# Two causal attentions in a two-layer network: row maxima by 64 queries, and turns moved by one chunk

## The reference

```python
scores = (einsum(q_cos, k_cos) + einsum(q_sin, k_sin)) / sqrt(8) * exp(log_scale)   # layer 0
scores = einsum('bhqd,bhkd->bhqk', q, k) / sqrt(8)                                    # layer 1
scores = where(causal, scores, -inf)
attn = softmax(scores, axis=-1)          # over 512 keys, exact maximum of each row
out = einsum('bhqk,bhkd->bhqd', attn, v) @ Wo.T
```

## Time and profile before

| | |
|---|---|
| runs | 1258.14, 1243.11 and 1254.38 us, median 1254.38 |
| the profiled execution | 1254.72 us, its span 1253.1 us |
| busy over the span | PE 79%, DVE 66%, ACT 54%, POOL 47% |
| `attend0`, from about 393 to 640 us | PE 225.8 of 247.0 us, DVE 224.5, ACT 185.0, POOL 114.1 |
| `attend1`, 973 to 1253 us | PE 246.3 of 280.0 us, DVE 233.6, ACT 195.0, POOL 183.8 |

### The profile page before, as it was taken

The page is one execution under the profiler, slowest core; times in us unless marked ns, Lnnn a source line. Parts: engine busy times, 40 slices in busy tenths (PEclk is TensorE's granted clock), DMA queues, the critical chain, the costliest instruction groups (busy, mean ns, idle before and its releaser), DMA issues. The chain is left out here.

```text
span 1253.1 us, 25971 instructions
## 1 busy us (share of the span) xinstructions
PE 996.1 (79%) x8908; PEld 650.2 (52%) x8908; DVE 832.1 (66%) x1875; ACT 680.5 (54%) x1293; POOL 586.7 (47%) x862
## 2 busy tenths in 40 slices
PE   3789753989874999999976463499999699999997
PEld 1456531777672455555533332388888345555542
DVE  1566331799986899999927666133333799999992
ACT  1266443776720777777755353122222377777774
POOL 3467537244432444455433466111110477777774
PEclk9899766899996899999997575699999599999998
DMA  4322032477775222222202233466664111112110
GB/s 135 110 49 54 27 100 89 139 206 201 217 156 132 70 70 70 70 73 77 61 7 63 76 106 96 146 183 192 190 184 136 43 45 53 53 53 53 53 47 27
DMA packets 151525, 122.57 MB, mean 98 GB/s; under 512 B 31712, under 2 KB 134032, under 8 KB 151408
## 3 DMA queue, kind: packets, MB, share of 16 engines
q1 hardware_dynamic: 141664, 102.89, 29.6%
q0 software_dynamic: 8016, 17.71, 4.9%
q10 hardware_dynamic: 1728, 0.46, 0.2%
HBM read 75.75 MB, written 42.61 MB: 94 GB/s over the span
## 5 line engine op out<-in xcount | busy, mean ns | idle before, releaser
L2103 ACT ACTIVATE attend_probs<-attend_attend_ps 128x512 f32<-128x512 f32 x640 | 353.7, 600 | 152.7 <-PE attend_attend_ps L2171 141.5
L2171 PE MATMUL attend_attend_ps<-attend_q,attend_ks 50*128 50x512 f16 (+3 forms) x1024 | 236.6, 307 | 23.1 <-ACT attend_probs L2103 20.3
L2070 POOL TENSOR_SCALAR_AFFINE_SELECT attend_probs<-attend_probs 128x512 f32<-128x512 f32 x256 | 159.6, 636 | 196.7 <-ACT attend_probs L2103 196.1
L2139 PE MATMUL attend_attend_ps<-attend_ks,attend_q 48*128 48x512 f16 (+3 forms) x1024 | 191.5, 317 | 27.8 <-DMA attend_ks<-k_stack 20.2
L2184 PE MATMUL attend_attend_ps<-attend_probs,attend_vals 128*32 128x512 f32 (+3 forms) x2048 | 183.2, 455 | 0.0
L2266 DVE TENSOR_REDUCE attend_neg_max<-attend_attend_ps 128x2 f32<-128x1024 f32 x128 | 155.5, 1215 | 14.3 <-PE attend_attend_ps L2151 9.0
L2151 PE MATMUL attend_attend_ps<-identb,stairs 64*128 64x128 bf16 (+1 forms) x1280 | 144.5, 213 | 0.0
L2171 PEld LDWEIGHTS attend_attend_ps<-attend_q,attend_ks 50*128 50x128 f16 x1024 | 70.4, 94 | 121.6 <-ACT attend_probs L2103 73.7
L2268 DVE TENSOR_REDUCE attend_neg_max<-attend_attend_ps 128x2 f32<-128x768 f32 x128 | 121.9, 952 | 8.2 <-PE attend_attend_ps L2151 7.3
L2151 PEld LDWEIGHTS attend_attend_ps<-identb,stairs 64*128 64x128 bf16 x1280 | 104.4, 100 | 19.3 <-issue 4.7
L1886 PE MATMUL experts_experts_ps<-experts_rowsT,experts_w_in 128*128 128x256 f32 (+1 forms) x468 | 110.2, 386 | 1.6 <-ACT experts_rowsT L1835 1.5
(11 more groups left out here) (316 smaller groups left out, 1933.4 us busy)
## 6 DMA issues: line engine op xcount, KB each, us to landing
experts_w_in<-in_L_ffn_w_dram SPq DMA_DIRECT2D x78, 176.0 KB, 2.4
q_stack<-middle_parts SPq DMA_DIRECT2D x24, 256.0 KB
k_stack<-middle_parts SPq DMA_DIRECT2D x24, 256.0 KB
attend_q<-q_stack SPq DMA_DIRECT2D x64, 96.0 KB
attend_ks<-k_stack SPq DMA_DIRECT2D x64, 96.0 KB
middle_w_in<-in_L_ffn_W_dram SPq DMA_DIRECT2D x23, 256.0 KB
middle_w_out<-in_L_ffn_W_dram SPq DMA_DIRECT2D x23, 256.0 KB
experts_rows<-sorted POOLq DMA_DIRECT2D x39, 128.0 KB, 2.5
```

Source lines behind the costliest of these rows:

```text
L2070: pool.affine_select(out=block_, in_=block_, compare_op=ALU.is_ge, fill=0.0, base=0, pattern=[[0, GH], [1, P]], channel_multiplier=-1).the ...
L2103: act.activation(probs[:, u.par, 2 * c + side, :], ps[:, PROB + side, :], ACT.Exp, scale=SCALE ** -2)\
L2139: pe.matmul(ps[:, bank + side, col:col + (qt + 1) * P], q[rows(side, KR), g, pair, qt * P:(qt + 1) * P], ks[rows(side, KR), g, pair, 0:(qt ...
L2171: mm = pe.matmul(ps[:, PROB + side, col:col + S - kt * P], ks[rows(side, KM), g, pair, kt * P:(kt + 1) * P], q[rows(side, KM), g, pair, kt ...
```

## The change

Maxima by 64 queries. Query blocks are now of `H` = 64 (`QS` = 8 a head). A block of 64 queries fills 64 of PE's columns, so a matmul of `maxima` fills a quarter of the array (64 rows by 64 columns); the four heads of the unit go to the four quarters. The two sides of one pair write the two partition halves of one and the same bank. A chunk covers one large and one small block of all four heads instead of one of two heads: 1024, 1024, 1024, 1024 and 512 elements a partition for DVE, where there were five times 1024. The mask's products are one instead of two per head and chunk. Each matmul of `probabilities` is now two, each with 64 of the 128 keys, into two partition halves of one bank. The layout of the maxima and their parts follows; the turn of the maxima is two matmuls instead of one.

Turns. PE turns the maxima of unit t - 1 in chunk 0, and the mix of unit t - 4 in chunk 1, behind the first piece of `mix`. DVE's copy of the maxima comes after the reduction of chunk 0, its `divide` after chunk 1's, and `add_row` moves from the end of a step to behind `split_maxima` of the next.

POOL. The copy of the values and the gathers of the feed-forward result stood before a unit's four masks, and the joins after them; now a gather and a join stand after the first mask, and the copy for the next unit, the second gather and the second join after the last.

```diff
         def max_chunk(c):
-            if c == 4:
-                return [(0, 1, 0), (1, 1, 256)]
-            return [(c // 2, 3, 0)] if c % 2 == 0 else [(c // 2, 2, 0), (c // 2, 0, 384)]
+            if c == 0:
+                return [(QS - 1, 0)]
+            return [(QS - 1 - c, 0), (c - 1, (QS - c) * H)] if c < 4 else [(3, 0)]
+        def half(side, pair):
+            first = H * ((side + pair) % 2)
+            return slice(first, first + H)
...
-            for n in range(UNITS + JOIN_AFTER * layer):
-                if n < UNITS:
...
+            copy_values(0)
+            for n in range(UNITS):
+                mask(n, 0)
+                gather(n, 0)
                 if layer == 1 and n >= JOIN_AFTER:
-                    join_branches(n - JOIN_AFTER)
+                    join_branch(n - JOIN_AFTER, 0)
+                for i in range(1, QT):
+                    mask(n, i)
+                if n + 1 < UNITS:
+                    copy_values(n + 1)
+                if layer == 1:
+                    gather(n, 1)
+                    if n >= JOIN_AFTER:
+                        join_branch(n - JOIN_AFTER, 1)
...
                 blocks = max_chunk(c)
-                for n, (pair, qt, col) in enumerate(blocks):
+                for n, (qs, col) in enumerate(blocks):
+                    for pair in range(HP):
+                        for side in range(2):
+                            pe.matmul(ps[half(side, pair), bank + pair, col:col + (qs + 1) * H],
+                                      q[rows(side, KR), g, pair, qs * H:(qs + 1) * H], ks[rows(side, KR), g, pair, 0:(qs + 1) * H],
+                                      start=(n == 0), stop=False)
...
                 for pair, kt, col in prob_chunk(c):
-                    mm = pe.matmul(ps[:, PROB + side, col:col + S - kt * P], ks[rows(side, KM), g, pair, kt * P:(kt + 1) * P],
-                                   q[rows(side, KM), g, pair, kt * P:S], start=True, stop=True)
+                    for first in (0, H):
+                        mm = pe.matmul(ps[first:first + H, PROB + side, col:col + S - kt * P],
+                                       ks[rows(side, KM), g, pair, kt * P + first:kt * P + first + H], q[rows(side, KM), g, pair, kt * P:S],
+                                       start=True, stop=True)
                 mm.then_inc(prob_ps.sem, 1)
...
+            def before_maxima(t):
+                if active(t, 5, UNITS):
+                    pe.wait_ge(context_done.sem, context_done.done(t - 5))
+                    if (t - 5).group == NG - 1:
+                        pe.wait_ge(added.sem, added.done((t - 5).row))
             def before_mix(t):
-                if active(t, 2, UNITS):
-                    pe.wait_ge(maxT_ready.sem, maxT_ready.done(t - 2))
-                elif active(t, 5, UNITS):
-                    pe.wait_ge(context_done.sem, context_done.done(t - 5))
-                if active(t, 5, UNITS) and (t - 5).group == NG - 1:
-                    pe.wait_ge(added.sem, added.done((t - 5).row))
-            def before_maxima(t):
-                if active(t, 4, UNITS):
-                    pe.wait_ge(context_done.sem, context_done.done(t - 4))
-                elif active(t, 2, UNITS):
-                    pe.wait_ge(maxT_ready.sem, maxT_ready.done(t - 2))
+                if active(t, 1, UNITS):
+                    pe.wait_ge(maxT_ready.sem, maxT_ready.done(t - 1))
+                else:
+                    before_maxima(t)
             def step(t):
                 row_ends = active(t, 4, UNITS) and (t - 4).group == NG - 1
                         maxima(t, c)
                     if active(t, 2, UNITS):
                         probabilities(t - 2, c, 1)
-                    if c == 0 and active(t, 4, UNITS):
-                        before_mix(t)
-                        turn_mix(t - 4)
+                    if c == 0 and active(t, 1, UNITS):
+                        before_maxima(t)
+                        turn_maxima(t - 1)
                     if 1 <= c <= 3 and active(t, 3, UNITS):
                         mix(t - 3, c - 1)
                         if c == 3:
                             mix(t - 3, 3)
-                    if c == 1 and active(t, 1, UNITS):
-                        before_maxima(t)
-                        turn_maxima(t - 1)
+                    if c == 1 and active(t, 4, UNITS):
+                        before_mix(t)
+                        turn_mix(t - 4)
                     if c == 2 and row_ends:
-                        if active(t, 1, UNITS):
-                            pe.wait_ge(maxT_ready.sem, maxT_ready.done(t - 1))
                         turn_context(t - 4)
...
             def reduce(u, c):
                 dve.wait_ge(scored.sem, scored.after(u, 2 * c + 1))
                 first = max_pair(u, c)
                 pair_banks = ps[:, first:first + 2, :]
-                out = neg_max[:, u.par, :, :, :]
-                if c == 4:
-                    ins = dve.tensor_reduce(out[:, :, :, 1], pair_banks.rearrange("p s (h t) -> p s h t", h=HP), X_AXIS, ALU.max,
-                                            negate=True)
-                elif c % 2 == 0:
-                    ins = dve.tensor_reduce(out[:, :, c // 2, 3], pair_banks, X_AXIS, ALU.max, negate=True)
-                else:
-                    dve.tensor_reduce(out[:, :, c // 2, 2], pair_banks[:, :, 0:384], X_AXIS, ALU.max, negate=True)
-                    ins = dve.tensor_reduce(out[:, :, c // 2, 0], pair_banks[:, :, 384:512], X_AXIS, ALU.max, negate=True)
+                for qs, col in max_chunk(c):
+                    ins = dve.tensor_reduce(neg_max[:, u.par, :, qs], pair_banks[:, :, col:col + (qs + 1) * H], X_AXIS, ALU.max, negate=True)
                 ins.then_inc(maxed.sem, 1)
...
             def step(t):
                 if active(t, 1, UNITS):
                     split_maxima(t - 1)
+                if active(t, 5, UNITS) and (t - 5).group == NG - 1:
+                    add_row(t - 5)
                 for c in range(MCH):
                     if active(t, 0, UNITS):
                         reduce(t, c)
-                    if c == 0 and active(t, 4, UNITS):
+                    if c == 0 and active(t, 1, UNITS):
+                        copy_maxima(t - 1)
+                    if c == 1 and active(t, 4, UNITS):
                         divide(t - 4)
-                    if c == 1 and active(t, 1, UNITS):
-                        copy_maxima(t - 1)
-                if active(t, 4, UNITS) and (t - 4).group == NG - 1:
-                    add_row(t - 4)
```

110 lines of the change are left out of this document (55 added, 55 removed).

## The result

The changed kernel takes 1307.56 us (median of 1298.23 to 1309.54), the kernel before 1251.57 in the same comparison: ratio 1.046 (1.041 to 1.050). The forecast was 1270 us, with a range of 1252 to 1293. The profiled execution took 1306.94 us, its span 1305.3, 52.2 more than before.

A forecast was written before the change was run, and what follows sets the result against it. The closed PE-ACT loop was taken as the bound, DVE's loop having hardly more slack. `attend0` +12.0, `attend1` +3.9, first steps -2.6 and `attend1`'s extra +2 made +15.3 on 1254.72: 1270 us, range 1252 to 1293.

The forecast's parts named there:

- POOL: nothing: POOL's new order of gathers, joins and copies: claimed to cost nothing, each mask being used one step later.
- off the new loop: `attend1`'s delays from DVE's slower split, late `divide` and turn: claimed off the new loop, so its row is also 31.82 us.
- Nothing below is a matter of the clock: PE's granted clock, 1.00 in the steady part of both attentions before: claimed to play no part, no time counted.
- the forecast's +15.3: Whole kernel: the summed slowdown in us, added to the profiled execution's 1254.72.
- The closed loop through PE and ACT, not DVE, is the bound: A step of `attend0`: PE and ACT waiting on each other sum to 7.23 us, the whole step, without slack.
- Transposes +0.55, from 1.03 to 1.58: From `mix`'s first piece to chunk 2: the moved transposes lengthen this stretch of the loop by 0.55 us a step.
- Quarters run side by side, -0.05: Maxima in chunk 3: quarter-array matmuls run side by side, fewer columns saving 0.05 us a step on the loop.
- the step of 7.73: New normal step in us, claimed for both attentions: 7.23 + 0.55 - 0.05.
- End of a batch row 0.90: End of each four-step batch row: 0.59 us for the context's transposes plus 0.31 for the projection, 1.18 before.
- the whole extra of 1.16 us a row: `attend1`'s longer row before the change, put down to DVE's slower split; a quarter, +2 us, was kept on the loop.
- First three steps -2.6: First three steps of each attention, without a mix: DVE sets the pace and saves 6 x 0.43 us.
- two sides in one bank: Rival, chance 0.25: lower rows' maxima need 0.21 us more in chunks 2 and 3; step 8.15, kernel 1294 us.

The follow-up runs named there:

- the first trace: The changed kernel unaltered, as first profiled, against the kernel before: ratio 1.046, rows of 33.2 us in `attend0` and 34.5 in `attend1`.
- e2: The changed kernel with PE's and DVE's order of the turns put back as before; ratio 1.000 to the kernel before.
- e3: The kernel before with only the turns moved as in the change (PE's and DVE's order); ratio 1.052 to the kernel before.
- e5: The changed kernel unaltered, run again on chip 6; ratio 1.037 to the kernel before on that chip.
- e14: The changed kernel with plain DMAs in place of the indirect gathers, on chip 13; ratio 1.025 to the kernel before.
- e12: The changed kernel with the mix's four transposes also issued in chunk 0, ahead of the turn of the maxima; ratio 1.048 to the kernel before.
- e6: The kernel before, unaltered, on chip 6 as the reference (ratio 1); rows of 30.08 us in `attend0` and 30.46 in `attend1`.

## Why the prediction was wrong, step by step

Two steps failed, each of them a term put at nothing. *"POOL: nothing"*, with `attend1`'s delays "off the new loop", left out what the gathers do to PE's signals: 25 us in the first trace (how much of it POOL's new order brought stays open). *"Nothing below is a matter of the clock"* left out its falls, 9 us. Together they are 34 of the 37 us between the forecast's +15.3 and the measured +52.2. The loop and the price of the transposes, which the forecast rests on, were right. Step by step:

- *The closed loop through PE and ACT, not DVE, is the bound*: right. DVE's 0.43 us a step less gained nothing by itself (e2), and DVE waits now. Without these 0.43 (e3) it hands over the split late enough to cost 0.1.
- *Transposes +0.55, from 1.03 to 1.58*: right to the hundredth. It is 0.55 of the 0.58 us by which the step grew where no signal was late (e5's 7.81), and e2 takes it back.
- *Quarters run side by side, -0.05*: the mechanism is right, the size is +0.03: chunk 2 takes 0.63 to 0.64 instead of 0.61, chunk 3 0.64 instead of 0.62, and chunk 4 0.45 to ACT's start instead of 0.42. With these 0.08 the step of 7.73 is the 7.81 of e5 and e14. At the full clock a weight load of 64 columns shows 105 ns (e12, 420.7 to 662.1), more than the 93 of 128 columns that I took for both; whether that is the 0.08 was not tested apart:

```profile
L2198 PEld LDWEIGHTS attend_attend_ps<-attend_q,attend_ks 50*64 50x64 f16 x894 | 37.3, 105 | 59.1 <-issue 32.7 <-ACT attend_probs L2129 21.7
```

   The rule of the Trainium skill (TensorEngine Tiling (Array Packing), Gotcha 1) that different row tiles can't access one bank at a time did not show as a cost: two sides write one bank, and a chunk is longer than forecast by 0.02 to 0.03 us at most.
- *End of a batch row 0.90*: it is 8.40 + 8.07 - 2 x 7.81 = 0.85. The row came to 32.09, forecast 31.82.
- *"Nothing below is a matter of the clock"*: failed. It was read from the kernel before, where it holds. The transposes were counted as hidden work that costs nothing to take away; they were also what kept PE busy while it waits, and without them the clock falls. Against the row of 33.2 and 34.5, the falls are 238.5 - 7 x 33.2 = 6 us and 244.2 - 7 x 34.5 = 3.
- *"POOL: nothing"*, and *"these delays are off the new loop"*: failed on the chips with late signals, the first among them. The gathers meet chunk 2's signals, which the loop waits for: 33.2 and 34.5 instead of 32.09, so 8 + 17 = 25 us. The kernel before had its own in `attend1`, where I put the whole extra of 1.16 us a row down to DVE's split: 0.36 are the split's and 0.80 late signals. The prediction kept 2 us of the extra for the loop; what it missed is that two thirds of it were no delay of DVE.
- *First three steps -2.6*: near. From the first reduction to unit 3's split both attentions together take 2.2 us less. The sum has no term for the tail, and behind unit 31's split `attend1` alone takes 31.2 instead of 27.9 us.

The sum as it should have been: `attend0` 7 x (32.09 - 30.10) = +13.9 (forecast +12.0), `attend1` 7 x (32.09 - 31.26) = +5.8 (+5.9), all else -1.0 (-2.6): 18.7. With 9 for the clock and 25 for the signals it is 53, and 52.2 were measured. The rival "two sides in one bank" came nearest in microseconds, by luck: its 8.15 us is near the 8.2 of the first trace, but its 0.21 in chunk 2 is not there, and the delay of chunk 3 is a signal's.

Even where no signal was late (e5), the ratio was 1.037, 1298 us on the first chip, above the range too. Its two stretches are 19.9 and 15.8 us longer than e6's; 7 x 2.01 and 7 x 1.63 of that are the row (30.08 and 30.46 to 32.09), 10.2 the falls. All else takes 3.7 more.

## What to carry over

Ask of work that lies in an engine's wait not only what it costs but what it does there: on PE it also holds the clock, and moving it away costs twice, once where it lands and once by the hole. When a trace shows two consumers starting late by the same amount behind a matmul that had ended, look at what another engine was doing just then, and run the unaltered kernel on another chip before believing in a cause. Work saved on an engine off the loop is worth nothing until the loop is shortened by as much.
